# Second feed-forward of chunks 0 to 2 placed inside the attention of later chunks, with block outputs turned by VectorE

## What is computed

```python
x = x + 0.5 * ffn(layernorm(x))          # first feed-forward
x = x + attn(layernorm(x))               # attention, 16 heads of 8, page-causal (pages of 32)
x = x + 0.5 * ffn(layernorm(x))          # second feed-forward, the same weights

def ffn(x):
    y1 = ln(x + mha(x)) * g1 + b1        # mha over sequences of one token: a linear map
    gates = softmax(y1 @ wg); idx = argmax(gates)      # one of 8 experts
    keep = (rank of the token among those of its expert) < 256
    moe = where(keep, gate * ((y1 @ w1[idx] + b1[idx]) @ w2[idx] + b2[idx]), 0)
    return ln(y1 + moe) * g2 + b2
```

## Time and profile before

| | us |
|---|---|
| median of 3 runs | 495.75 |
| lowest, highest | 492.46, 503.6 |
| the profiled execution | 495.45 |
| its span | 493.7 |
| granted TensorE clock, mean | 0.925 |

### The profile page before, as it was taken

How to read it: one execution, slowest core, us unless ns; L and a number is a source line. 1 busy time by engine, 2 the same in 40 slices (tenths; PEclk the granted TensorE clock), 3 DMA queues, 4 the chain that set the end, 5 groups by cost and what they waited for, 6 DMA issues and landing times.

```text
span 493.7 us, 7548 instructions
## 1 busy us (share of the span) xinstructions
PE 391.1 (79%) x2749; PEld 150.2 (30%) x2749; DVE 167.9 (34%) x631; ACT 356.5 (72%) x551; POOL 110.4 (22%) x203
## 2 busy tenths in 40 slices
PE   2799999236661898888888888888888887789990
PEld 1798544122220222222121121111121111655540
DVE  2524487639666031111010010101010000668885
ACT  1324567435231899999999999999999998356761
POOL 2532578830000000000000000000000000477785
PEclk9869999759775799999999999999999999999996
DMA  6930920001888980000000000000000000000001
GB/s 134 385 147 15 115 33 1 0 1 64 180 217 212 230 132 3 2 1 1 1 1 1 0 2 1 1 0 1 2 0 1 1 0 2 1 0 3 21 23 42
DMA packets 23172, 24.44 MB, mean 50 GB/s; under 512 B 2364, under 2 KB 20348, under 8 KB 22876
## 3 DMA queue, kind: packets, MB, share of 16 engines
q1 hardware_dynamic: 23132, 23.92, 20.7%
HBM read 16.51 MB, written 7.41 MB: 48 GB/s over the span
## 4 chain that ended last, share of the span: by engine, by line
ACT 26%; PE 19%; issue 18%; DVE 9%; POOL 3%; DVEq 0%; ACTq 0%; POOLq 0%
ACT arena L543 24%; PE ps L1025 7%; PE ps L1009 3%; PE ps L1034 2%; PE ps L947 2%; PE ps L922 1%; DVE arena L716 1%; PE ps L926 1%; DVE longest L700 1%; DVE stats L553 1%; DVE arena L729 1%; ACT arena L507 1%; DVE arena L734 1%; POOL arena L444 1%; PE ps L857 1%
## 5 line engine op out<-in xcount | busy, mean ns | idle before, releaser
L543 ACT ACTIVATE arena<-ps 128x1024 f32<-128x1024 f32 x272 | 251.3, 1129 | 13.4 <-PE ps L1009 13.3
L1025 PE MATMUL ps<-arena,v_st 128*9 128x512 f32 (+3 forms) x1280 | 144.8, 534 | 29.0 <-ACT arena L543 28.9
L1009 PE MATMUL ps<-packed 51*128 51x512 bf16 (+4 forms) x640 | 85.2, 353 | 5.6 <-issue 5.3
L435 POOL TENSOR_TENSOR arena<-x_tm,lnb 128x512 f32<-128x512 f32 x8 | 10.0, 1267 | 317.2 <-DVE x_tm L571 317.1
L776 DVE COPY o_sb<-ps 128x512 f32<-128x512 f32 x16 | 11.1, 692 | 187.4 <-PE ps L1025 187.4
L1009 PEld LDWEIGHTS ps<-packed 51*128 51x128 bf16 (+1 forms) x640 | 20.4, 95 | 106.0 <-ACT arena L543 94.9
L1025 PEld LDWEIGHTS ps<-arena,v_st 128*9 128x9 f32 x1280 | 20.6, 89 | 97.3 <-ACT arena L543 86.9
L507 ACT ACTIVATE arena<-ps,arena 128x128 f32<-128x128 f32 x128 | 36.1, 367 | 11.5 <-PE ps L922 10.3
L646 DVE SCALAR_TENSOR_TENSOR arena<-ps,arena 128x128 f32<-128x128 f32 x128 | 35.3, 343 | 13.2 <-ACT arena L507 7.7
L926 PE MATMUL ps<-w,arena 128*128 128x512 f32 x64 | 33.1, 599 | 0.4 <-DVE arena L646 0.3
L922 PE MATMUL ps<-w,arena 128*128 128x512 f32 x64 | 33.2, 601 | 0.1
(11 more groups left out here) (119 smaller groups left out, 397.8 us busy)
## 6 DMA issues: line engine op xcount, KB each, us to landing
packed<-piece_dram SPq DMA_DIRECT2D x16, 384.0 KB
piece_dram<-arena SPq DMA_DIRECT2D x8, 384.0 KB, 6.8
packed<-in_w1T SPq DMA_DIRECT2D x8, 256.0 KB, 4.7
packed<-in_w SPq DMA_DIRECT2D x8, 256.0 KB, 4.9
trio<-in_rope SPq DMA_DIRECT2D x2, 1024.0 KB, 7.9
piece_dram<-arena SPq DMA_DIRECT2D x8, 256.0 KB, 6.8
packed<-in_template SPq DMA_DIRECT2D x4, 480.0 KB, 12.5
x_tm<-in_x SPq DMA_DIRECT2D x4, 256.0 KB, 5.0
```

The lines of the kernel that those rows point to most:

```text
L543: nc.scalar.activation(pexp[:, n % PB, :], ps[:, at:at + 2, :].rearrange("p b n -> p (b n)"), ACT.Exp, scale=SCALE).then_inc(exp_done, 1)
L1009: ins = pe.matmul(ps[:, 2 * (n % SLOTS) + b, col:col + w], packed[rows, 1, pair, P * j:P * (j + 1)], packed[rows, 0, pair, q:q + w], start ...
L1025: ins = pe.matmul(ps[32 * h:32 * h + VW, 6 + k % OB, q - GW * c:q - GW * c + w], v_st[:, j, GH * g + h, :], pexp[:, n % PB, 512 * b + col: ...
```

## The change

Chunks 0 to 2 of the second feed-forward are taken out of its ORDER (only chunk 3 stays) and become 48 steps, 16 a chunk: O A P C L R K B and, for each of four tiles, H (high experts) and E (low experts). Each is tied to one group: of the seven groups of a block of chunk 1 those numbered 1, 3, 5; of the eleven of chunk 2's 1, 3, 5, 9; of the fifteen of chunk 3's 1, 3, 6, 9, 12. TensorE runs the step behind `values` of that group, in the output bank that the running block doesn't use. It first waits until VectorE has read the step before (`early_read`) or, for the first step in a block, has turned the last block's output; the first `values` of a block waits for the read of the step before, too. So chunk 0 goes from block 4 to 8, chunk 1 from 9 to 12, chunk 2 from 12 to 15.

VectorE does what ScalarE did of these steps (the copies of A, C, K, B, the scaling of H); GpSimd normalises LN1 and LN2 and does F. Only the exponential of the gates stays on ScalarE, placed behind the exponential of the unit LAST_UNIT[m] + 5 (EXP_AFTER). A block's output is turned by VectorE alone, in 32x32 blocks, straight from PSUM; the fourth block of a chunk is followed by a second such turn, of 128x512, that gives the chunk's oT by features. `turn_output` and the steps U are gone. The rows of wo are loaded by four DMAs in the order that this gives. The buffers of the second feed-forward have places of their own (the piece buffers and the sin and cos tables), so GpSimd and VectorE wait once for the stores of the pieces. Results of chunks 0 to 2 are stored when they are there.

```diff
+EARLY = G - 1
+SLOT_AT = {1: (1, 3, 5), 2: (1, 3, 5, 9), 3: (1, 3, 6, 9, 12)}
+SLOT_GROUPS = [min(m for m in range(len(GROUPS)) if GROUPS[m][0] == k) + at
+               for k in range(NG, len(BLOCKS)) for at in SLOT_AT[BLOCKS[k][0]]]
+EARLY_STEPS = [(step, i) for g in range(EARLY)
+               for step, i in [(s, g) for s in "OAPCLRKB"] + [(s, t) for t in range(GT * g, GT * (g + 1)) for s in "HE"]]
+EARLY_AT = list(zip(SLOT_GROUPS, EARLY_STEPS))
+EARLY_BANK = {step: 7 - GROUPS[m][0] % OB for m, step in EARLY_AT}
+EXP_AFTER = {LAST_UNIT[m] + SLOTS + 2: i for m, (step, i) in EARLY_AT if step == "L"}
...
+        "pe": "O3 A3 P3 C3 L3 R3 K3 B3 E12 E13 E14 E15",
+        "act": "A3 M3 C3 L3 K3 B3 E12 E13 E14 E15",
+        "dve": "O3 X3 P3 L3 R3 K3 E12 E13 E14 E15 Z3 F3",
+        "pool": "X3 P3 B3 E12 E13 E14 E15 Z3",
...
+            for h in range(GH):
+                sp.dma_start(wqo[VC * h:VC * (h + 1), 1, :],
+                             a["wo"].rearrange("(g h d) n -> h g d n", g=NG, h=GH)[h]).then_inc(wo_in, 16)
...
+            pool.wait_ge(piece_out, 16 * 2 * STORE_DMAS * G)
+            for g in range(EARLY):
+                ln_rsqrt(ROWS, 1, g)
+                add_bias(1, g)
+                ln_rsqrt(LN1, 1, g)
+                normalise(LN1, 1, g)
+                for t in range(GT * g, GT * (g + 1)):
+                    add_experts(1, t)
+                ln_rsqrt(LN2, 1, g)
+                normalise(LN2, 1, g)
+                pool.wait_ge(normed[LN2], EARLY + g + 1)
+                pool.tensor_tensor(y[:, group(g), :], y[:, group(g), :], rows_of(lnb[:, 0, :]), ALU.mult).then_inc(z_part, 1)
+                pool.wait_ge(z_part, G + g + 1)
+                pool.wait_ge(xb_ready, G + g + 1)
+                pool.tensor_tensor(x_tm[:, group(g), :], y[:, group(g), :], xb[1][:, group(g), :], ALU.add).then_inc(x_new[2], 1)
             feed_forward(1)
...
+            def take_output(k):
+                c, g = BLOCKS[k]
                 dve.wait_ge(pv_done, LAST_GROUP[k] + 1)
-                dve.tensor_copy(o_sb[:, b, :], ps[:, 6 + b, :]).then_inc(o_copied, 1)
+                if k:
+                    dve.wait_ge(o_read, k)
+                dve.transpose(o_t[:].rearrange("p t v -> p (t v)"), ps[:, 6 + k % OB, :]).then_inc(o_turned, 1)
                 dve.wait_ge(o_turned, k + 1)
+                dve.reciprocal(den[:], o_t[:, :, HD]).then_inc(den_ready, 1)
                 dve.wait_ge(den_ready, k + 1)
+                if g == 0 and c:
+                    dve.wait_ge(copied[OUT], c)
+                dve.tensor_tensor(attn_n[:, :, HD * g:HD * (g + 1)], o_t[:, :, 0:HD],
+                                  den[:].unsqueeze(2).to_broadcast([P, GW // VC, HD]), ALU.mult).then_inc(o_read, 1)
+                if g == NG - 1:
+                    dve.wait_ge(o_read, k + 1)
+                    dve.transpose(oT[:, cols(c)], attn_n[:].rearrange("p t v -> p (t v)")).then_inc(copied[OUT], 1)
...
+            for m in range(len(GROUPS)):
+                if m in LAST_GROUP:
+                    take_output(LAST_GROUP.index(m))
+                for at, (step, i) in EARLY_AT:
+                    if at == m:
+                        if step == "R":
+                            pick_expert(1, i)
+                        if step == "O" and i:
+                            out_stats(1, i - 1)
+                        early(step, i)
+            out_stats(1, EARLY - 1)
             feed_forward(1)
...
+            def early(at, step, i):
+                bank, k = EARLY_BANK[step, i], GROUPS[EARLY_AT[at][0]][0]
+                if at and GROUPS[EARLY_AT[at - 1][0]][0] == k:
+                    early_read(*EARLY_AT[at - 1][1])
+                else:
+                    pe.wait_ge(o_turned, k)
...
             for m in range(len(GROUPS)):
                 while done < min(LAST_UNIT[m] + SLOTS, len(UNITS)):
                     scores(done)
                     done += 1
                 values(m)
-                if m in turning:
-                    turn_output(turning[m])
+                for at, (where, (step, i)) in enumerate(EARLY_AT):
+                    if where == m:
+                        early(at, step, i)
+            early_read(*EARLY_AT[-1][1])
             feed_forward(1)
```

More of the change, by code:

```diff
@@ L789, in _ @@
         def _(pe):
-            def turn(kind, g, src):
-                for k in range(GT):
-                    ins = pe.transpose(ps[:, CHAIN + g % 2, P * k:P * (k + 1)], src[:, GT * g + k, :], ident[:])
-                ins.then_inc(turned[kind], 1)
             def by_tile(bank, g, lhs, rhs, done):
@@ L811, in misc_free, with turn_rows, project_out @@
                     pe.wait_ge(misc_read[last], of + 1)
+            def turn_rows(kind, g, src, bank):
+                for k in range(GT):
+                    ins = pe.transpose(ps[:, bank, P * k:P * (k + 1)], src[:, GT * g + k, :], ident[:])
+                ins.then_inc(turned[kind], 1)
+            def project_out(g, bank):
+                pe.wait_ge(copied[OUT], g + 1)
+                if g == 0:
+                    pe.wait_ge(wo_in, 16 * GH)
+                by_tile(bank, g, oT, wqo[:, 1, :], out_mm)
@@ new lines, in mha, with logits @@
+            def mha(n, g, bank):
+                if n == 0:
+                    pe.wait_ge(prep_dve, 4)
+                pe.wait_ge(copied[ROWS], G * n + g + 1)
+                by_tile(bank, g, xT, w_mha[:], mha_mm)
+            def logits(n, g, bank):
+                pe.wait_ge(copied[Y1], G * n + g + 1)
+                if n == 0:
+                    pe.wait_ge(route_in, 16 * ROUTE)
+                for t in range(GT * g, GT * (g + 1)):
+                    ins = pe.matmul(ps[:, bank, E * t:E * (t + 1)], y1T[n][:, P * t:P * (t + 1)], wg[:],
+                                    start=True, stop=True)
+                ins.then_inc(logit_mm, 1)
@@ new lines, in places @@
+            def places(n, g, bank):
+                pe.wait_ge(pick_ready, 2 * (G * n + g) + 1)
+                first, end = GT * g, GT * (g + 1)
+                pe.matmul(ps[:, bank, P + E * first:P + E * end], tri_bf[:, 0, :], pick_bf[:, E * first:E * end],
+                          start=True, stop=False)
+                for back in range(1, end):
+                    at = max(first, back)
+                    ins = pe.matmul(ps[:, bank, P + E * at:P + E * end], tri_bf[:, 1, :],
+                                    pick_bf[:, E * (at - back):E * (end - back)], start=False, stop=(back == end - 1))
+                ins.then_inc(place_mm, 1)
@@ new lines, in turn_coef, with bias @@
+            def turn_coef(n, g, bank):
+                pe.wait_ge(coef_ready, G * n + g + 1)
+                pe.transpose(ps[0:TE, bank, P * (2 + g % 2):P * (3 + g % 2)],
+                             coef[n][:, group(g), :].rearrange("p t e -> p (t e)"), ident[:]).then_inc(coef_mm, 1)
+            def bias(n, g, bank):
+                pe.wait_ge(coefT_ready, G * n + g + 1)
+                pe.matmul(ps[:, bank, :], coefT[:, g, :], b12_big[:].rearrange("p t d -> p (t d)"), start=True, stop=False)
+                for k in range(GT):
+                    n0 = P * (GT * g + k)
+                    ins = pe.matmul(ps[:, bank, D * k:D * (k + 1)], y1T[n][:, n0:n0 + P], ident[:],
+                                    start=False, stop=(k == GT - 1))
+                ins.then_inc(bias_mm, 1)
@@ L813, in feed_forward, with experts @@
+            def experts(n, t, high, bank):
+                pe.matmul(ps[:, bank, :], y1T[n][:, P * t:P * (t + 1)], w12[:, 512 * high:512 * (high + 1)],
+                          start=True, stop=True).then_inc(high_mm if high else low_mm, 1)
             def feed_forward(n):
@@ L854, in feed_forward @@
[L854 to L870 removed]
+                        logits(n, g, MISC)
+                    elif step == "R":
+                        places(n, g, MISC)
```

390 lines of the change are left out of this document (219 added, 171 removed), and 8 rows, old and new, of the table ORDER.

## The result

The changed kernel takes 499.75 us, median of 4 runs (499.58 to 511.0); the kernel before took 495.01 beside it (492.46 to 503.6). The ratio is 1.0104, with a 95% interval of 1.0056 to 1.0152: about 1% slower, no difference by the 2% bound, where 498.7 was forecast. Some executions, of the kernel before too, are 8 to 12 us longer; they are left out of the ratios, and in the three profiles that are of such an execution (the first of the changed kernel, that of the turns alone, that of the eight products) the first stage is what is longer, 170.1 to 171.2, so that only their later stages are read. The rows here are from a second profile of the changed kernel, run as the first experiment: 499.52 us, span 497.7.

A forecast was written before the change was run, and what follows sets the result against it. ScalarE paces attention, TensorE close behind. Span 493.7 plus 31.6 in attention less 28.4 in the last stage gives 496.9, with 1.75 around it 498.7 us, 0.6% slower; own range 491 to 505.

The forecast's parts named there:

- The bound and the law: Attention: ScalarE sets the pace; a TensorE piece of length X costs it X - 0.25 us, never won back.
- the expert piece: Attention: each H or E product lasts 0.86 us and costs ScalarE 0.61, eight times a chunk.
- The wait for the stores of the pieces: Start of attention: already met, as the packed rows that attention needs come behind these stores; no cost.
- P to C: Attention: VectorE's and GpSimd's chain between these steps takes 7.0 us, making chunks 0 and 2 late; +4.5 (3.7 to 8.1).
- L to R: Attention: the gates' exponential and VectorE's choice make R late, by 1.15 us in chunks 0 and 1; +2.2 in all.
- further waits: Attention: every step has one or two waits more than its matmuls; 1.0 us taken, from nothing to 2.9.
- The last stage: Behind attention: one chunk's chain of 47.4 us in place of 75.8, so -28.4.
- The clock: Last stage: TensorE idles, its clock falls to 1.2 GHz, and C, L, R, B and one expert piece double; +4.7 us.
- the wait for X3: Last stage: chunk 3's 1/sqrt queues behind chunk 2's work on GpSimd, ready at 11.9; 5 us in the open.
- Filled gaps: Rival, attention: pieces fill TensorE's idle time first, attention grows by 12.4, time 479.5 us; chance 0.16.
- The clock falls inside attention: Rival, attention: TensorE's stops before C and R drop its clock to 1.2 GHz, time 512 us; chance 0.24.
- No queue before X3: Rival, last stage: chunk 2's statistics come early enough, the 5 us in the open go, 493.7 us; chance 0.1.

The follow-up runs named there:

- the turns alone: Against the kernel before: block outputs turned by VectorE in 32x32 blocks, no early steps, all four chunks behind attention; 487.66 to 489.62 us, ratio 0.989.
- the eight products: Changed kernel with chunk 3's 1/sqrt moved ahead, plus eight unread TensorE products in the last stage, seven behind P3 and one behind L3; 497.01 us.
- the first experiment: The changed kernel, unaltered, run again for a profile of an undisturbed execution; 499.52 us.
- the halved pieces: Changed kernel with columns 256 to 511 of each of the 24 early expert products not computed; 489.0 to 489.32 us, ratio 0.9914.

## Why the prediction was right, step by step

**The bound and the law held.** ScalarE sets attention's pace, and a piece costs its length less 0.25: the halved pieces (0.79 to 0.36) show slope 1 and slack 0.26, and the steps that no wait makes late agree: A 0.32 (0.33 forecast), L 0.72 (0.65), O and P 0.82 and 0.83 (0.75), B 1.87 (1.8).

**One term was mis-sized: the expert piece.** The step "H and E are 0.86 and cost 0.61, eight times a chunk" took the length from a stretch of the earlier trace rows where such pieces follow each other. Between value products it is 1.05, and the loss 0.79: 24 x 0.18 = +4.3.

**One wait was put at nothing.** "The wait for the stores of the pieces is met, as the packed rows that attention needs come behind them" holds for the rows of the first scores. The last stores are issued from 159.5 on, behind the first exponential at 158.6, and land at 171.6; VectorE waits for them before its first turn, and this cost 1.5 in the changed kernel's profile.

**The other waits.** P to C: place, releaser and sign as forecast; 3.3, not 4.5, since GpSimd's tile took 0.448, not 0.6. L to R: R lost 0.9, 1.0 and 0.2 in the three chunks, 2.1 with its own length, where 2.5 was forecast for R and K together; the gates moved forward gave 1.7 back. The 1.0 for further waits shows as some 0.07 on each O, P, L and B, 0.8 in all.

The account of attention closes. The steps that I count on ScalarE come to 39.0, the wait for the stores to 1.5, and the turns give 4.9 back: 35.6. Against the forecast the terms are off by +4.3, +1.5, -1.2, -0.4 and -0.2, together the 4.0 that attention missed by. So the forecast of attention is better than its parts: two losses that it didn't have were in part made up by waits that it counted too dear.

**The last stage.** -28.4 forecast, -28.3 measured. P3 starts 11.4 after the last values (11.9; the terms as written add up to 11.7). From there to the end of B it is 17.6 (14.1 and 3.85 of half clock), the expert pieces take 8.3 (7.7 with the one at half clock), and from their end on it is 10.2 (9.8). The clock is worth 4.5 (4.7). Two things inside it were otherwise. Less of the wait for X3 was in the open, 3.3 where 5 was forecast, as half clock already held up P3's product, which the sum had at the full clock. And it doesn't follow that without the queue the 5 would go: moved, the 1/sqrt gave 3.2.

**The rivals.** *Filled gaps* needed a loss under 0.3 a piece; it was 0.79. *The clock falls inside attention* needed a long stop before C; 2.06 came, and the clock stayed at 1.00 through it. *No queue before X3* is out, as the 1/sqrt ended P3's wait.

**Luck.** The forecast of 498.7 came within 1.1 of the 499.75, and that is nearer than its parts: attention was 4.0 longer than forecast, and in the profiled execution the first stage, which the forecast left as it was, 3.3 shorter. As a difference, 3.25 was forecast against the profiled execution of before; the ratio gives some 5.2.

Where the expected gain went is shown from two sides: three chunks cost 40.5 in attention and gave 28.3 behind it (12.2 lost), and the turns, which had to be made for it, gave 4.9 back. Stage by stage this is +7.3; the times themselves differ by 1.04%, some 5.2, and the rest lies in the first stage, whose variation between executions is of that size.

## What to carry to other kernels

Idle time of an engine that feeds the pacing engine is not room: what counts is the slack at the one place where a piece goes in, here 0.26 us a group of 1.83, and what is longer comes out as lost time in full. Price work at the margin in both places before moving it: the last chunk moved cost 12.8 in attention, and took 8.7 off the stage behind it. For every wait that a change adds, ask when its last condition comes true, and what the engine that waits would have done by then. Take a piece's length from a neighbourhood like the one that it will stand in, with what comes on top between pieces of different kinds, and time the parts of a change that can stand alone by themselves; one of them may be the gain.

## What the runs showed of the hardware

- An fp32 product of 128x512 takes 1.05 from start to start when it follows the value products, and 0.86 between products of the same kind; a half one takes 0.63, so that 0.20 of it doesn't depend on the columns. That it is the weight load (0.19) in the open is likely by the trace, and not shown.
- In the kernel with the turns alone the granted clock fell to 1.2 GHz behind a stretch in which TensorE was idle half the time (busy 1.47 of 3.00), with no stop over 1.02 in it, and stayed there through 6.5 us in which TensorE was busy without a pause. The Trainium skill (TensorE: Matmul & The Clock Gate, Part 1) has activity release the throttled clock; here activity did, but only later.
- The same work and stops of TensorE behind attention were followed by a fall of the clock between 454 and 455 in the changed kernel, some 4 behind the last values, and by none until 461, 8 behind them, in the kernel with the 1/sqrt moved.
- The clock stayed at 1.00 with products that nobody reads ahead of the waits (44.3 to 39.3 in one kernel, 75.8 to 73.3 in another). Begun once it had fallen, such products brought it back and gained nothing (44.4), as they stood in the way and it fell again behind them.
- VectorE turns 128x512 fp32 from PSUM in 32x32 blocks in 0.712, at the price of a copy (0.692); GpSimd scales and shifts 128x128 with scalars by partition in 0.448.
